# A Mamba-2 block between two expert layers: the cumulative sums of a group, one slot later

## The reference

```
x = x + 0.5 * ffn(layernorm(x))
x = x + mamba2(layernorm(x))
x = x + 0.5 * ffn(layernorm(x))
```

```
z, xBC, dt = split(x @ W_in)               # 512, 640 and 8 columns
dt  = softplus(dt + dt_bias)               # one value for each token and head
xBC = silu(conv(xBC, conv_w) + conv_b)     # 4 taps along the sequence
x_ssm, B, C = split(xBC)                   # 8 heads x 64, 64, 64
state = state * exp(dt * A) + dt * x_ssm * B      # token by token
y = state . C + D * x_ssm
y = y * silu(z); y = y * rsqrt(mean(y*y) + eps) * norm_weight
out = y @ W_out
```

## Time and profile before

| what | us |
|---|---|
| runs | 1306.03, 1306.69, 1313.96 |
| median | 1306.69 |
| profiled execution, device time | 1312.65 |
| profiled execution, span of the trace | 1310.9 |

### The profile page before, as it was taken

One profiled execution on the slowest core, in us unless ns is written; L12 is line 12 of the kernel. 1 busy time (PEld: TensorE's weight loads), 2 busy tenths in 40 slices (PEclk: granted clock), 3 DMA queues, 4 the chain that ended last, 5 costly groups with the idle time before them and its releaser, 6 DMA issues. The chain is left out here.

```text
span 1310.9 us, 21923 instructions
## 1 busy us (share of the span) xinstructions
PE 1062.4 (81%) x6532; PEld 883.3 (67%) x6532; DVE 809.1 (62%) x1611; ACT 618.4 (47%) x1494; POOL 655.7 (50%) x593
## 2 busy tenths in 40 slices
PE   3747999999916788999999999989747999999900
PEld 3646999999914566766666666657536999999800
DVE  6974444444437898698989897875383444444434
ACT  1333555555513565556565656564333555555400
POOL 6913555555421465556565655567505555555300
PEclk9998999999966888788988888899868999999955
DMA  6861222222232111111111100000062222222178
GB/s 230 267 273 49 78 77 77 78 77 78 58 109 73 49 37 41 37 45 35 47 41 42 41 25 17 17 17 25 29 257 65 77 77 78 77 77 76 53 243 275
DMA packets 73242, 112.20 MB, mean 86 GB/s; under 512 B 10664, under 2 KB 60336, under 8 KB 71856
## 3 DMA queue, kind: packets, MB, share of 16 engines
q1 hardware_dynamic: 47888, 58.77, 13.2%
q0 software_dynamic: 13824, 37.77, 8.8%
q10 hardware_dynamic: 11424, 14.30, 3.2%
HBM read 66.76 MB, written 44.04 MB: 85 GB/s over the span
## 5 line engine op out<-in xcount | busy, mean ns | idle before, releaser
L399 POOL DMA_INDIRECT ys_d<-xs,row_of x144 | 142.0, 986 | 195.3 <-DVE xs L779 189.5
L768 DVE TENSOR_TENSOR xl<-pT,xh 128x256 fp32r<-128x256 f32 x144 | 61.1, 424 | 223.9 <-ACT xh L476 223.9
L394 POOL DMA_INDIRECT xs<-xn_d,token_of x144 | 139.8, 971 | 114.4 <-DVE token_of L753 71.2
L463 ACT ACTIVATE hs<-pH 128x512 f32<-128x512 f32 x144 | 86.0, 597 | 233.8 <-PE pH L581 233.8
L773 DVE TENSOR_TENSOR h2l<-hs,h2h 128x512 fp32r<-128x512 f32 x144 | 99.8, 693 | 78.0 <-ACT h2h L471 77.8
L1548 DVE SCALAR_TENSOR_TENSOR acc<-raw,cwh,acc 128x512 f32<-128x512 f32 x104 | 120.9, 1208 | 2.2 <-POOL acc L1075 1.2
L1171 ACT ACTIVATE ex<-bank,dts 128x128 f32<-128x128 f32 x256 | 72.5, 366 | 98.9 <-PE bank L1316 98.9
L601 PE MATMUL pY<-w2h,h2h 128*128 x576 | 102.8, 300 | 0.5 <-DVE h2l L773 0.3
L1060 POOL TENSOR_TENSOR yv<-yv,sz 128x512 f32<-128x512 f32 x32 | 48.0, 1501 | 95.8 <-DVE yv L1598 95.8
L581 PE MATMUL pH<-w1h,xh 128*128 x288 | 92.7, 404 | 1.8 <-DVE xl L768 1.1
L581 PE MATMUL pH<-w1l,xh 128*128 x288 | 92.7, 404 | 0.0
(11 more groups left out here) (248 smaller groups left out, 2668.8 us busy)
## 6 DMA issues: line engine op xcount, KB each, us to landing
m_yg<-ys_d SPq DMA_DIRECT2D x64, 128.0 KB, 2.1
xs<-ys_d SPq DMA_DIRECT2D x16, 512.0 KB, 6.0
wst<-in_L_ffn_w_dram ACTq DMA_DIRECT2D x8, 512.0 KB, 4.7
xs<-in_L_attn_x_dram SPq DMA_DIRECT2D x8, 512.0 KB, 6.6
hs<-in_L_ffn_w_dram ACTq DMA_DIRECT2D x8, 512.0 KB, 5.0
xn_d<-xs SPq DMA_DIRECT2D x8, 512.0 KB, 3.2
lo_d<-w1l SPq DMA_DIRECT2D x1, 4096.0 KB, 11.8
lo_d<-w2l SPq DMA_DIRECT2D x1, 4096.0 KB, 21.3
```

The costliest lines, as they stand in the source:

```text
L394: pool.indirect_dma_start(out=xg[:, t % NX, :], out_offset=None, in_=xn_d, in_offset=bass.IndirectOffsetOnAxis(ap=token_of[:, t:t + 1], ax ...
L399: pool.indirect_dma_start(out=ys_d, out_offset=bass.IndirectOffsetOnAxis(ap=row_of[:, t:t + 1], axis=0), in_=y[:, t % NX, :], in_offset=No ...
L463: act.activation(r[:, u, :], pH[u][:, :], ACT.Relu).then_inc(relu_done.sem, 1)
```

## The change

The function that says in which slot a group's sums are taken up, cum_group, moves from slot 0 to slot 1 of the group before. So sum_up and weigh (VectorE), the two exponentials, the copy and the exponential of dec (ScalarE) move from slot 0 to slot 1, and the two copies of the remainders (ScalarE) from slot 1 to slot 2. The three matmuls of the sums move from the end of slot 3 to the end of slot 0. As the bank must not be written while VectorE reads it, dt's product of slot 0 moves from late to early in its slot, that of slot 1 from early to late, and turn_b's wait for dec_in moves from slot 0 to slot 1. Nothing is added or removed, and no DMA moves.

```diff
         def cum_group(s):
 
             G = s // GC + 1
-            return G if s % GC == 0 and 0 <= G < NG else None
+            return G if s % GC == 1 and 0 <= G < NG else None
@@ turn_b
                 if k == 0 and G + 1 < NG:
                     pe.wait_ge(dt_added.sem, dt_added.done(G + 1))
-                if k == 1 and G + 1 < NG:
+                if k == 2 and G + 1 < NG:
                     pe.wait_ge(dec_in.sem, dec_in.done(G + 1))
@@ TensorE's list of a slot
-                if live(s + 8) and s % GC != 0:
+                if live(s + 8) and s % GC != 1:
                     project_dt(s + 8, s)
...
-                if live(s + 8) and s % GC == 0:
+                if live(s + 8) and s % GC == 1:
                     if cum_group(s) is not None:
                         pe.wait_ge(dec_in.sem, dec_in.done(cum_group(s)))
                     project_dt(s + 8, s + 1)
                 if live(s - 2):
                     turn_x2(s - 2, s)
-                G = soft_group(s)
+                G = cum_group(s + 1)
                 if G is not None:
                     pe.wait_ge(a_done.sem, a_done.done(G))
                     pe.wait_ge(bt_done.sem, bt_done.done(s + 1))
```

## The result

The changed kernel takes 1315.09 us (median of 20 runs, 1311.72 to 1321.00), the kernel before 1308.98 us (20 runs, 1306.03 to 1317.56). The ratio is 1.0043, 95% interval 1.0029 to 1.0057: about 6 us slower, where I had forecast 6 us faster. The profiled execution after took 1314.96 us, near its median.

The account below looks back on a forecast made before the run. The prediction took VectorE's queue to bound slot 0, with room in slot 1. Six gains of 1.2 us (7.2) plus 0.3 for slot 24, less 1.4 for slots 1, gave -6.1 us: 1300.5 us, range 1290 to 1309.

Parts of the forecast that it names:

- The gain of 1.2 us: Slot 0: L1606 starting 0.6 us sooner, taps 0.5 shorter, weigh's product gone 0.1; 1.2 us a group.
- 6.93 forecast: Slot 0: VectorE's six convolution taps would take 6.93 us against 7.41, a gain of 0.5 us.
- Group 0's sums: Made before slot 0 with no state work around them; counted as no gain.
- I take the wait as free in the short ones: Slot 1, short kind: B transpose's 1.6 us wait for dec_in is repaid, slots 1 and 2 together keeping their length.
- Seven slots 1 cost 7 x 0.2 = 1.4: Slots 1: weigh at the slot's end plus a 0.1 us wait, 0.2 us a group, 1.4 us in all.
- slot 1 has room on it: Slot 1: VectorE's queue has room, being busy 10.13 of 13.28 us.
- TensorE then only arrives sooner at the transpose that waits for dec_in; I count nothing: Slot 1: the dt product, up to 1.00 us, leaves TensorE's front; counted as no gain.
- The wait is not repaid: Rival: short slots 1 grow by 1.6 us and slot 2 stays; 1305 us, no visible change. Chance 0.21.
- Slower: the wait lowers the clock: Rival: TensorE idling before L1294 in slot 1 lowers its clock; 15 us slower, 1322 us. Chance 0.05.
- GpSimd's stall: Rival: slot 0's stall around GpSimd's L1060 comes more often, 6.7 us each; one gives 1307, two 1314. Chance 0.09.
- TensorE's clock gains: Rival: filling TensorE's holes around slot 1 removes low-clock stretches, 12 us more gain, 1289 us. Chance 0.13.
- a larger gain for the taps in slot 0: Slot 0: by the port-pair rule the taps gain up to 1.0 us instead of 0.5; sum 3 us lower, 1297.5.

Follow-up runs that it names:

- e8: Kernel before with five small linked VectorE instructions, results unused, in front of L1598 in slot 1; no wait added, sums left in slot 0. Ratio to before 1.0025.
- e6: Kernel before with one wait added: TensorE's B transpose in slot 1 waits for the end of VectorE's L1598. Ratio to before 1.0028.
- e9: Changed kernel with ScalarE reading all three sums from the shared bank early in slot 1, so the B transpose no longer waits for sum_up. Ratio to before 0.9986.
- e3: Changed kernel with sum_up moved forward in VectorE's slot 1, right behind scale_state. Ratio to before 1.0025.
- e10: e9 with sum_up also behind the taps of slot 1, and the decay's exponential and weigh one slot later. Ratio to before 0.9907, median 1297.22 us.
- e2: Changed kernel with 12 unused TensorE transposes in slot 1, in front of the product within the tile. Ratio to before 1.0064.
- e4: Changed kernel with slot 1's first projection in front of the product within the tile. Ratio to before 0.9986, median 1308.62 us.
- e7: e4 with slot 1's dt product in front of turn_x instead of at the slot's end. Ratio to before 0.9988.
- e11: e10 with slot 1's first projection in front of the product within the tile. Ratio to before 0.9923, median 1299.97 us.
- e1: Kernel before with only slot 1's dt product moved late in its slot; sums and their wait unmoved. Ratio to before 1.0000.

## Why the prediction was wrong

**Right: slot 0.** The gain of 1.2 us was measured as 1.23 (mean of five), and by the steps given: L1606 waits for L1273, and the six taps take 6.72 instead of 7.41 us (6.93 forecast). One term put at nothing was a gain: "Group 0's sums". The block's slot 0 begins at 444.1 to 445.5 us in the eight kernels that have the change, and at 446.6 to 446.9 in five of the six that do not (445.24 in e8).

**Wrong: "I take the wait as free in the short ones".** This is the step that failed. The wait came as sized (1.55 us against 1.6, slot 13 13.51 us), though in two groups of the trace (slots 13 and 21), not three, and it was not repaid in slot 2. I had read off the equal sums of rows 3 that a short slot 1 is followed by a long slot 2, and inferred that lengthening the one shortens the other. In that trace the two go with where the low clock fell: the short slots 1 (1, 13, 17) hold about 1 us of it and the slots 2 behind them 4.5 to 5.6, the long ones (9, 21) 3.6 and the slots behind 0 to 2.7. Lengthening slot 1 by a wait left slot 2 longer, 19.42 us after 13.51; in e6 one pair of three repaid it. e6, the wait alone, costs 0.28%; e9, the change without it, gets 0.57% back.

**Wrong: "Seven slots 1 cost 7 x 0.2 = 1.4".** The 1.06 us of sum_up in slot 1 stand in no term of the sum; "slot 1 has room on it" was to cover them. e8, the work alone, costs 0.25%, 1.05 us in a slot without low clock. The queue in front of L1598 is also GpSimd's and TensorE's turn_y, which I had not followed; and VectorE's instructions behind took longer beside GpSimd's products, which had moved later too.

The two, 0.28 and 0.25% (0.53), less the gain of slot 0 (six times 1.2 us, 0.55%), would give no change at all, so they do not add up to +0.43%. Part of the rest is seen, in a term that I had put at nothing: "TensorE then only arrives sooner at the transpose that waits for dec_in; I count nothing". It arrives sooner at L1264 too, and in slots 9 and 17 it idles there for 1.6 us; four of the six slots 1 have the low clock (15.0 to 15.3 us). The wait does not cause that: the same slots of 14.9 to 15.4 us stand in e3, e9 and e10, where TensorE does not wait for dec_in. Ten slots 1 of the changed kernel, e3, e9 and e10 have the hole of 1.6 us in front of that product, and all ten last 14.9 to 15.2 us at 0.77 or 0.78; where work was put into it (e2, e4, e7, e11) slots 1 are 12.9 to 13.5 us long but for one. Some low slots 1 come without it (slots 1 and 5 of the changed kernel, slot 1 of e1 and e10, slot 5 of e9), and a hole of 1.1 us in slot 1 of e9 brought no low clock. What the low clock of slots 1 costs the whole stays open, as filling the hole moved part of it to slots 2, and e2 gained nothing. Slots 14 and 22 hold about 8 us of it each.

**The rivals.** "The wait is not repaid" was the one that came, but at 1305 it was priced 10 us too low, since the work and the clock were left out of it. "Slower: the wait lowers the clock" (0.05) had the sign and the slot right and the mechanism wrong: the two slots 1 with over 1 us of idle time in front of L1294 kept clocks of 0.95 and 0.94, and the low ones have it in front of L1264 or not at all. Its 15 us were too many. GpSimd's stall of the earlier trace rows did not occur in the profile after, where no L1060 takes over 1.67 us. "TensorE's clock gains" fell: over slots 0 to 23 the mean clock is 0.88 after and 0.89 before, with less of the low clock in slots 0 and about twice as much in slots 1.

The Trainium skill's rule on the port pair (SBUF — State Buffer, "SBUF: two separate sides") gave a larger gain for the taps in slot 0 than was measured, 1.0 against 0.7 us. It fits e8 better: the variance of 0.15 us that is recorded with 1.01 ends with the GpSimd product of 1.49 us that had begun before it.

**What stays open.** The two clusters of e10, what sets in which slot of a group the granted clock falls, and how much of the +0.43% it costs.

## What to carry to other kernels

When work moves from a bound slot to one with room, follow everything queued behind its new place on the other engines: here GpSimd's next product and a wait on a shared PSUM bank, together worth as much as the gain. Let the engine that idles at that moment read the shared bank, and put the rest of the work where the queue really waits; the same move then gained 0.7% by the medians (0.3 to 1.1% with the intervals) instead of losing 0.4%. A negative correlation between neighbouring slots in one trace is not a promise that lengthening one shortens the other.

## What was not expected of the hardware

TensorE's low clock behaved like something that is passed on: filling a 1.6 us hole with transposes (e2) left slots 1 with at most 3.5 us of it, and in three groups put 6 to 8 us of it into the slot 2 behind, where the changed kernel had 0 to 2. A VectorE instruction on 3 values a partition, 0.15 us alone, was recorded with 1.01 us when it began 0.5 us into a GpSimd product of 1.49, and ended with it.
